# A two-layer decoder on one core: where the inner projection, the convolution and the couplings stand

## The reference

```python
x = ln(x + L0_attn(x))        # random features: exp(x W - |x|^2 c) times a fixed matrix
x = ln(x + L0_xattn(x, ctx))  # 16 heads of cross attention, softmax over 120 keys
x = ln(x + L0_ffn(x))         # coupling net, below
x = ln(x + L1_attn(x))        # selective scan, below
x = ln(x + L1_xattn(x, ctx))  # out = (gelu(x ctx^T) * (x ctx^T)) ctx, gated attention
x = ln(x + L1_ffn(x))         # mixture of 8 experts, the best one alone, times its probability
```

```python
# L0_ffn, three cycles
gf = global_net(mean over s)                       # one number per batch
for _ in range(3):
    tf = coupling_net(out)                         # four layers, one number per row
    coupling = 0.1 + range * (0.7 * gf + 0.3 * tf - 0.5) * 2
    out = out + coupling * twist(out)
# L1_attn, inner width 512, 16 states
x_ssm, res = split(x @ W_in.T)                     # two halves of 512
xc = silu(conv4(x_ssm))                            # four taps along s
delta = softplus(xc); A_d = exp(delta * A)
h = A_d * h + xc * xc                              # along s, for each of 16 states
y = (xc * sum_states(h)) * silu(res) + D * xc
out = y @ W_out.T
# L1_ffn
probs = softmax(x @ router_w + router_b)
y = max(probs) * expert[argmax(probs)](x)          # the first one, where several are equal
```

## Time and profile before

| | |
|---|---|
| runs | 3101.62, 3106.39, 3107.36 us; median 3106.39 |
| the profiled execution, its span | 3099.29 us, 3097.5 us |
| busy: PE, DVE, ACT, POOL | 2540.1 (82%), 2495.3 (81%), 1727.8 (56%), 1487.4 us (48%) |
| TensorE's mean granted clock | 0.872 |
| the chain that ended last | PE 47%, DVE 28%, issue 14%, ACT 7% |
| 64 scans on VectorE | 1.20 us each |
| transfers | 4% of the DMA engines' span |

### The profile page before, as it was taken

The page is one execution under the profiler, slowest core; times in us unless marked ns, Lnnn a source line. Parts: engine busy times, 40 slices in busy tenths (PEclk is TensorE's granted clock), DMA queues, the critical chain, the costliest instruction groups (busy, mean ns, idle before and its releaser), DMA issues.

```text
span 3097.5 us, 41602 instructions
## 1 busy us (share of the span) xinstructions
PE 2540.1 (82%) x11020; PEld 1469.9 (47%) x11020; DVE 2495.3 (81%) x4288; ACT 1727.8 (56%) x3062; POOL 1487.4 (48%) x1159
## 2 busy tenths in 40 slices
PE   6896888979888897888988788888888889887556
PEld 3544554544444454445545444554544445454323
DVE  2368888897978889898888978788897888978783
ACT  1457564646657474665646466564656646465620
POOL 1046354554535455563545545354553545456460
PEclk7868888888989989999898899898898989978687
DMA  3000000000000000000000000000000000000000
GB/s 131 10 8 10 14 11 14 17 14 7 10 21 10 14 17 14 7 10 21 10 14 13 18 7 10 21 10 14 13 3 21 10 14 7 7 7 1 14 7 7
DMA packets 16849, 45.72 MB, mean 15 GB/s; under 512 B 2248, under 2 KB 7056, under 8 KB 16400
## 3 DMA queue, kind: packets, MB, share of 16 engines
q1 hardware_dynamic: 16656, 43.96, 4.2%
HBM read 35.57 MB, written 8.39 MB: 14 GB/s over the span
## 4 chain that ended last, share of the span: by engine, by line
PE 47%; DVE 28%; issue 14%; ACT 7%; DVEq 2%; POOL 1%; ACTq 0%; DMA 0%; SPq 0%; POOLq 0%
PE bank L535 45%; DVE h_ring L1087 14%; DVE x L1199 3%; DVE ln_stats L387 2%; DVE smax L991 1%; POOL ysum L1671 1%; ACT a_ring L1479 1%; DVE x L405 1%; DVE xpad L1093 1%; PE bank L413 1%; DVE soft L1066 1%; ACT L1485 1%; ACT L1339 1%; DVE ln_mv L391 1%; ACT spare L1420 1%
## 5 line engine op out<-in xcount | busy, mean ns | idle before, releaser
L1671 POOL TENSOR_TENSOR ysum<-ysum,h_ring 128x512 f32<-128x512 f32 x896 | 1155.2, 1289 | 633.3 <-DVE h_ring L1087 571.3
L1087 DVE TENSOR_TENSOR_SCAN h_ring<-a_ring,bank 128x512 f32<-128x512 f32 x1024 | 1172.7, 1200 | 27.2 <-ACT bank L1474 16.2
L1479 ACT ACTIVATE a_ring<-soft,decay 128x510 f32<-128x510 f32 x1024 | 675.7, 717 | 198.4 <-DVE h_ring L1087 198.0
L535 PE MATMUL bank<-w_expert_w,x45T 128*128 128x512 f32 x1024 | 541.1, 675 | 199.0 <-DVE x L1199 191.4
L535 PEld LDWEIGHTS bank<-w_expert_w,x45T 128*128 128x128 f32 x1024 | 213.2, 216 | 490.9 <-DVE x L1199 253.5
L1658 POOL TENSOR_TENSOR soft<-xc,soft 128x512 f32<-128x512 f32 x64 | 81.0, 1276 | 655.2 <-ACT soft L1457 655.2
L535 PE MATMUL bank<-x3T,w_winT 128*128 128x512 f32 x512 | 291.0, 704 | 39.7 <-ACT x3T L419 31.4
L991 DVE TENSOR_REDUCE smax<-bank 128x4 f32<-128x480 f32 x256 | 156.4, 652 | 143.1 <-PE bank L535 143.1
L535 PE MATMUL bank<-qT,kmask 32*120 32x256 f32 x1024 | 207.2, 497 | 50.2 <-ACT spare L1386 40.6
L535 PE MATMUL bank<-spare,w_cn_w 128*128 128x256 f32 x768 | 217.7, 408 | 37.0 <-ACT spare L1416 22.4
L1199 DVE SCALAR_TENSOR_TENSOR x<-bank,weight,x 128x256 f32<-128x256 f32 x512 | 212.5, 474 | 40.4 <-PE bank L535 40.4
(11 more groups left out here) (149 smaller groups left out, 3890.2 us busy)
## 6 DMA issues: line engine op xcount, KB each, us to landing
x0T<-in_xT SPq DMA_DIRECT2D x16, 512.0 KB, 3.3
x<-in_x SPq DMA_DIRECT2D x16, 512.0 KB, 4.3
out<-x SPq DMA_DIRECT2D x16, 512.0 KB, 3.0
ctxT<-in_ctxT SPq DMA_DIRECT2D x16, 240.0 KB, 2.5
ctxTb<-in_ctxT SPq DMA_DIRECT2D x16, 240.0 KB, 2.7
ctxb<-in_ctx SPq DMA_DIRECT2D x16, 240.0 KB, 3.0
w_expert_w<-in_expert_w SPq DMA_DIRECT2D x1, 2048.0 KB
w_winT<-in_winT SPq DMA_DIRECT2D x1, 1024.0 KB
```

The source lines that it names most:

```text
L535: return pe.matmul(o, l, r, start=start, stop=stop)
L1087: scanned.then(v.tensor_tensor_scan(h_ring[:, k % HRING, :], a_ring[:, k % RING, :, :].rearrange("p b s -> p (b s)"), xc2, 0.0, ALU.mult, ...
L1479: a.activation(a_ring[:, k % RING, :, 1:S], delta[:, c, :].rearrange("p (b s) -> p b s", b=NB)[:, :, 1:S], ACT.Exp, scale=decay[:, k:k + 1 ...
L1671: p.tensor_tensor(out=total, in0=first, in1=h_ring[:, k % HRING, :], op=ALU.add)\
```

## The change

Four things, in every turn:

1. *The inner projection.* The order of its units becomes 0, 1, 4, 5, 2, 3, 6, 7 in other banks. After the queries come units 0 and 1, two gates (4, 5) between the first scores, then the gated input product, then scores 2 to 7 in one run, then input 2, the transposes of the maxima, input 3 and the weighing. Gates 6 and 7 leave the head; they stand behind cycle 2, after expert unit 9, and wait there for the cycle's gates, whose banks they use. Before cycle 3 TensorE waits until ScalarE has read them.
2. *The convolution of inputs 2 and 3* goes from the head to the attention, after scan 8; their silu and softplus on ScalarE go behind `invert_sums(f, 1)`, with a pair of table loads of their own, and GpSimd's scan inputs for channels 2 and 3 behind additions 21 and 24. Silu of gates 6 and 7 gets a pair of table loads behind cycle 2; all in all ScalarE loads one table more in a turn, 12 for 11.
3. *The couplings* and their base move from VectorE to ScalarE: `couple = gate * gate_scale + base`, one activation behind each gate.
4. *The expert choice* no longer looks for the largest probability. The logits have their maximum subtracted already, so the best is where the logit is 0; rank and choice are made of that directly behind the logits, and its probability is 1 / sum.

```diff
-DELTA_AFTER = {13: 2, 18: 3}
+DELTA_AFTER = {21: 2, 24: 3}
-SQUARE_AT = (0, 18, 38, 59)
+SQUARE_AT = (0, 18, 36, 59)
...
-        IN = [bank[k][:, :] for k in (4, 5, 4, 5, 4, 5, 7, 4)]
+        IN_ORDER = (0, 1, 4, 5, 2, 3, 6, 7)
+        IN = [bank[k][:, :] for k in (4, 5, 4, 5, 7, 5, 0, 1)]
...
# TensorE, mamba_in
+                    elif k == 5:
+                        pe.wait_ge(in_read.sem, in_read.at(g, 4))
+                    elif k in (2, 3):
+                        pe.wait_ge(in_read.sem, in_read.at(g, k - 1))
+                    elif k >= 6 and f is not None:
+                        pe.wait_ge(gate_ready.sem, gate_ready.at(f, NB + k - 5))
...
# TensorE, turn, behind cycle 2
-                    experts(b, 9, 12)
+                    experts(b, 9, 10)
+                if m is not None:
+                    mamba_in(m, f, b, 6, 8)
+                if b is not None:
+                    experts(b, 10, 12)
...
+                if m is not None:
+                    pe.wait_ge(in_read.sem, in_read.at(m, 2 * IC))
                 if f is not None:
                     cycle(f, 2 * NB)
...
# VectorE, rotate
-                v.wait_ge(gate_ready.sem, gate_ready.at(g, s + 1))
-                cyc_chain.link(v.tensor_scalar(couple[:, b, :], gate[:, b, :], gate_scale[:, :], base[:, b:b + 1],
-                                               ALU.mult, ALU.add))
+                v.wait_ge(couple_ready.sem, couple_ready.at(g, s + 1))
...
# VectorE, route
+                pick_chain.link(v.scalar_tensor_tensor(out=prank[:, :, :], in0=logit[:, :, :], scalar=0.0,
+                                                       in1=over_tiles(row("rank")), op0=ALU.is_equal, op1=ALU.mult))
+                pick_chain.link(v.tensor_reduce(rmax[:, :], prank[:, :, :], AX, ALU.max))
+                pick_chain.then(v.tensor_tensor(out=pick[:, :, :], in0=prank[:, :, :], in1=over_experts(rmax[:, :]),
+                                                op=ALU.is_equal))
...
# VectorE, turn
+                if f is not None:
+                    maxima(f, 0, 1)
                 if m is not None:
                     convolve(m, 0)
                 if f is not None:
-                    maxima(f, 0, 2)
-                if m is not None:
-                    convolve(m, 2)
-                if f is not None:
-                    maxima(f, 2, 8)
+                    maxima(f, 1, 8)
...
+                states(m, 9)
+                if m is not None:
+                    convolve(m, 2)
                 states(m, 12)
...
# ScalarE, network
+                    a.activation(couple[:, b, :], gate[:, b, :], ACT.Identity, bias=base[:, b:b + 1],
+                                 scale=gate_scale[:, :]).then_inc(couple_ready.sem, 1)
...
# ScalarE, turn, behind invert_sums(f, 1)
+                if m is not None:
+                    silu()
+                    silu_conv(m, 2, IC)
+                    nat()
...
# GpSimd, before the product with res
+                    p.wait_ge(in_read.sem, in_read.at(g, gate_place(c) + 1))
```

More of the change, by code:

```diff
@@ L1536, in turn_ @@
                 nat()
+                if m is not None:
+                    softplus(m, 0, 2)
+                    decays(m, 6)
+                    mamba_in(m, 4, 6)
                 if f is not None:
@@ L1573, in turn_ @@
                     invert_sums(f, 1)
+                if m is not None:
+                    silu()
+                    silu_conv(m, 2, IC)
+                    nat()
                 if b is not None:
                     copy_weights(b)
+                if m is not None:
+                    softplus(m, 2, IC)
                 decays(m, 24)
@@ L1591, in turn_ @@
                     nat()
+                decays(m, 38)
                 if nxt is not None:
@@ L1596, in turn_ @@
                     cycle(f, NB)
-                    nat()
+                if m is not None:
+                    silu()
+                    mamba_in(m, 6, 8)
+                nat()
                 decays(m, STEPS)
```

120 lines of the change are left out of this document (46 added, 74 removed).

## The result

The changed kernel takes 3114.44 us (median of 11 runs, 3108.43 to 3124.72), the kernel before 3103.25 us (11 runs, 3094.59 to 3107.36). The ratio is 1.0039, with a 95% interval from 1.0025 to 1.0053: slower by 11 us. The sign and the range of the forecast (3070 to 3190) held, its size did not: 38 us were forecast. The profiled execution has a span of 3111.5 us, 14.0 more than before.

What follows compares the result with a forecast made beforehand. Bounds: TensorE in the head, VectorE in the attention, both alternately in the cycles. Terms −2.0 + 4.4 + 0.4 + 0.3 − 0.4 + 0 = +2.7 us a turn, times 14 = +38 on 3106.4: 3144 us, range 3070 to 3190.

Steps and rivals of the forecast that it cites:

- Step A: Head: three projection units leave or change place, so the first softmax comes earlier; −2.0 us a turn (−3.1 to +0.2).
- rival 1: Head: the clock stays up in the run of scores, the turn −3.3 us, 3060 us in all; chance 0.25.
- rival 2: Gain and loss cancel: clock returns with the unit behind the run, convolution unhindered; 3100 to 3112 us; chance 0.14.
- Step B: Attention, VectorE: convolution counts in full plus one wait on GpSimd, less the shorter choice; +4.4 us a turn (3.2 to 7.1).
- Rival 3: Attention: every convolution step waits for a GpSimd addition; +9.1 us a turn, 3271 us; chance 0.05.
- C: Attention: TensorE waits about 4.9 us for the context product, which may lower its clock; +0.4 us a turn (0 to 3).
- D: ScalarE behind the second inversion of sums: table loads and six activations, mostly covered by a wait; +0.3 us (0 to 1).
- Step E: Cycles: couplings leave VectorE, only the second of a pair can gain; −0.4 us a turn (−0.8 to +0.3).
- F: Behind cycle 2: two gate units, 3.8 us, covered by TensorE's 4.21 us wait for VectorE; 0 (up to +0.5).
- The incomplete turns cancel: Outside the 14 full turns: one without expert choice loses 1.7 us more, one without front gains as much.

Runs made afterwards that it cites:

- e8: Changed kernel with the two projection units behind the score run (inputs 2 and 3) put ahead of it: 3169 us, ratio 1.0233 to the kernel before.
- e5: e1 with VectorE's convolution of inputs 2 and 3 moved behind the second context product, in place of two scans that go later: 3068 us.
- e7: e1 with both the convolution behind the second context product and the second norm's reciprocal root ahead of softplus: 3009 us.
- e3: Changed kernel with the convolution of inputs 2 and 3, its silu and softplus back in the head, gates 4 and 5 between the scores: 3093 us.
- e1: Changed kernel with ScalarE's second convolution silu, its table loads and the softplus put behind two more decays and the next group's first feature: 3076 us.
- e4: Changed kernel with the couplings and their base back on VectorE: 3127 us, ratio 1.0078 to the kernel before.
- f3: Changed kernel with VectorE adding the last pair of expert units six scans earlier, alone: 3075 us.
- e6: e1 with the second norm's reciprocal root ahead of softplus on ScalarE and VectorE normalizing ahead of the scan: 3073 us.

## Why the prediction was right in sign and wrong in size

- **Step A was too small: −5.2 us where −2.0 stood.** The run of scores, its price and the fall of the clock were right (13.6 us against 13.74), and nearly so the softmax that is no longer held: 38.8 us into the turn against 41.2 before, −2.5. The step that failed is the sentence "The end of the gated output product, 1821.93 + 3.78, moves with it": I kept the 6.8 us between first softmax and that end, in which the product takes 3.78 us, for a fixed distance, and it is 3.9 now. It was slow only because the clock was down. I had weighed the clock in the run (rival 1) and its return with the unit behind the run (rival 2, A at −3.9), but not what it does between the softmax and the gated output. The units behind the run bring the clock back, and the wait of 0.68 us for the softmax, where 2.15 to 2.42 stood, no longer loses it. e8 shows that without these units all of the head's gain is gone. What the shorter wait is worth by itself no run shows.
- **Step B was right.** The convolution costs 5.7 us and meets one addition (1.0 us against 1.2), the choice gives 2.1 against 1.7: +3.6 where +4.4 stood. But the reason was not put to the test. "The convolution's steps have two inputs too" holds for six of the eight, and while these six ran, GpSimd had no addition. The step that waited reads a single tensor, and in e5 four normalizations of a single tensor take 3.00 us, beside additions, that take 1.38 in e7 without one. So the Trainium skill's sentence on VectorE instructions with two SBUF inputs ("SBUF — State Buffer", section Who interferes with whom) doesn't explain this wait, and no run here shows whether the six would have waited. The same section of the Trainium skill says that a tensor_scalar step, of which kind these are, can also contend for the port that VectorE shares with GpSimd. The rows agree with that: of the two first steps one takes 0.46 us and the other 1.50, until 0.28 us after the addition's end. Rival 3 fell for the reason given: GpSimd has nothing to add while no scan is computed.
- **Steps C and D together were too small: +2.0 us to cycle 2, with E, where +0.3 stood.** C cost nothing: TensorE waits 4.45 us for the first context product and is at the low clock for some 12 us behind it (the mixing takes 1.08 us), but the second context product comes 15.2 us after the first, as in e3 (15.3), which has no convolution there. D failed, and the text held what refutes it: it priced "a scan that waits for one" of the queued decays at 0.3 us. I took the 8.62 us for which the feature, on ScalarE, waits for TensorE for cover of the whole block, without asking what stands between: the decays for the next scans are in the same queue, behind the block, and VectorE needs the first of them at once. The wait is 4.51 us. e1, which puts two decays and a feature ahead of the block, takes it to 0.36 us and the way to cycle 2 down by 1.5 of the 2.0 us. The remaining 0.5 us no run takes apart.
- **Step E was near: −0.4 against about −0.9 by e4**, loosely. So was F: the two units cost nothing where they stand, for the way to cycle 3 is 41.3 us in both kernels.
- **The end of the turn had no term at all, and costs 1.5 us.** f3 shows that it is the low clock behind a wait of TensorE for VectorE's last sum: with the sum earlier it is gone. How long that wait is follows from the row ahead of it. In each of the twelve loop turns of all the kernels that have the wait, the last pair of expert units and the wait take 7.98 or 7.99 us together (5.48 + 2.51 in the changed kernel's turn above, 6.19 + 1.80 in e1, 5.21 + 2.77 in e6). The granted clock falls while TensorE stands ahead of this pair (6.03 us in these three). In e1 it falls 1.8 us before the pair begins and is back 5.0 us into it, in e6 it falls 3.75 us before and is back 3.1 us into it; so e6's pair is shorter and its wait behind it longer. What sets the moment of the fall is not settled: it also moves when something 80 us earlier in the turn moves (e1, e6).
- **"The incomplete turns cancel" was wrong.** The forecast counts 14 turns alike and nothing else; by the twelve turns' +1.9 that would be +27 us, and the span grew by 14.0. Outside the twelve turns the program is 9.0 us shorter, although two full turns are among that (the first of the loop, 0.1 us longer, and the last full one, 2.0 shorter). Why, no run shows.

So the sum of +2.7 a turn against +1.9 is no near hit: −3.2 of gain missed in the head, −0.8 in the attention, +1.7 and +1.5 of loss missed behind it. That the sign held is luck, since these errors nearly cancel: e1, one edit away, is 0.8% faster than the kernel before. And 3114 us lies below the 3120 to 3170 of the forecast itself, next to the 3100 to 3112 of rival 2.

## What to carry to other kernels

A stretch that an engine hides is only hidden if what the others need next is not in the same queue behind it: before putting a block into a long wait, list what stands between the block and that wait's end, and issue that first. Where an engine's duration changes with its clock, a distance between two of its marks is not a constant of the code; look at what it did just before. Here two units of work behind a stretch of waits were worth 3.4 us a turn over the same two ahead of it (183.7 against 187.1). Two edits that each move the next wait to the other's place can be worth next to nothing alone and 2% together (e5, e6 and e7), so a wait that has only moved is a reason to go on, not to undo.

## What the runs showed of the hardware

The same instructions in another order cost 1.8% (e8 against the changed kernel), most of it by TensorE's clock: behind the score run 1.21 and 3.78 us for what takes 0.69 and 1.99, 4.1 of the 5.2 us that the head loses. And the clock's level at one place can be the same in every turn and yet differ between two kernels whose instructions on TensorE stand in the same order: e6 ends all of its loop turns at the low level (residual product 3.10 to 3.14 us, after a wait of 2.77 to 2.79) and e1 all of them at the high one (1.98, after 1.79 to 1.83), though e6 only makes a root and a normalization earlier, some 80 us ahead of that place. The link is in the rows: the granted clock falls at another moment of the same 6.03 us wait, so the pair of units behind it takes another time and leaves another wait.
